# Cross-attention and a two-step mixture of experts on one core: the bias of the experts' second layer moved into a product tile, broadcast operands in place of diagonal matrices, idle products near the end, and a new order of work

## The reference

```python
logits = _gelu(xf @ w_r1 + b_r1) @ w_r2 + b_r2
top_p, top_i = jax.lax.top_k(jax.nn.softmax(logits, axis=-1), K)      # K = 2 of E = 8 experts
for _ in range(NUM_ITER):                                             # 2
    ctx = jnp.concatenate([integrated, v], axis=-1)
    shared_ctrl = _gelu(ctx @ w_s1 + b_s1) @ w_s2 + b_s2
    x_shared, v_shared = _inl(shared_ctrl, integrated, v, mu)
    hidden = _gelu(jnp.einsum('tc,tch->th', ctx_e, w1) + b1)          # w1, b1, w2, b2 of the token's experts
    ctrl = jnp.einsum('th,tho->to', hidden, w2) + b2                  # 64 hidden units, 384 outputs
    x_r, v_r = _inl(ctrl, x_e, v_e, mu)
    ...                                                               # weighted mean over the two experts
    halt = jax.nn.sigmoid(_gelu(x_next @ w_h1 + b_h1) @ w_h2 + b_h2)
    refined = _gelu(x_next @ w_f1 + b_f1) @ w_f2 + b_f2
    integrated = integrated + halt * refined * integration_weight
    v = v_next
```

## Time and profile before

| | us |
|---|---|
| median of 3 runs (lowest to highest) | 394.82 (390.18 to 397.71) |
| the profiled execution | 394.98 |
| its span, first to last instruction | 393.2 |
| PE busy | 352.4 (90%) |
| DVE busy | 294.6 (75%) |
| ACT busy | 255.3 (65%) |
| POOL busy | 47.0 (12%) |

### The profile page before, as it was taken

The page is one execution under the profiler, slowest core; times in us unless marked ns, Lnnn a source line. Parts: engine busy times, 40 slices in busy tenths (PEclk is TensorE's granted clock), DMA queues, the critical chain, the costliest instruction groups (busy, mean ns, idle before and its releaser), DMA issues. The chain is left out here.

```text
span 393.2 us, 5555 instructions
## 1 busy us (share of the span) xinstructions
PE 352.4 (90%) x1627; PEld 217.9 (55%) x1627; DVE 294.6 (75%) x649; ACT 255.3 (65%) x429; POOL 47.0 (12%) x57
## 2 busy tenths in 40 slices
PE   4778999998888978899998899999999999999775
PEld 2234444344333534566764657767767777776553
DVE  7587978768463468999998895985993995795822
ACT  2553576685858667896958767957686684786321
POOL 8029400024040403200000000000000000000000
PEclk9999999999999599999999999999999999999966
DMA  4540000000000000000000000000000000001000
GB/s 115 130 126 3 4 3 2 1 6 0 6 1 2 1 1 0 2 0 0 3 0 0 2 0 2 2 0 0 2 0 1 3 27 0 2 0 28 1 28 27
DMA packets 10667, 5.17 MB, mean 13 GB/s; under 512 B 4264, under 2 KB 10573, under 8 KB 10637
## 3 DMA queue, kind: packets, MB, share of 16 engines
q1 hardware_dynamic: 10637, 4.82, 4.6%
HBM read 3.64 MB, written 1.05 MB: 12 GB/s over the span
## 5 line engine op out<-in xcount | busy, mean ns | idle before, releaser
L674 PE MATMUL bank<-qs,w_hi 128*128 128x512 f32 x160 | 70.7, 442 | 0.0
L675 PE MATMUL bank<-qs,w_lo 128*128 128x512 f32 x160 | 63.1, 394 | 0.0
L850 ACT ACT_TABLE_LOAD x37 | 47.5, 1283 | 1.4 <-PEq L1346 0.7
L922 ACT ACTIVATE PT<-bank 77x512 f32<-77x512 f32 x64 | 35.4, 589 | 17.0 <-PE bank L779 9.6
L679 PE MATMUL bank<-KB,w_hi 128*128 128x512 f32 x160 | 43.7, 394 | 0.0
L961 ACT ACTIVATE hid<-bank,cols 128x512 f32<-128x512 f32 x40 | 27.0, 692 | 18.2 <-PE bank L640 18.0
L674 PEld LDWEIGHTS bank<-qs,w_hi 128*128 128x128 f32 x160 | 30.4, 190 | 7.8 <-ACT shared L967 1.0
L1234 DVE SCALAR_TENSOR_TENSOR masked<-Ib,cst,hid 128x512 f32<-128x512 bf16 x32 | 23.2, 750 | 15.1 <-ACT hid L961 15.1
L790 PE MATMUL bank<-PT,VO 77*32 77x512 f32 x256 | 34.3, 629 | 0.0
L679 PEld LDWEIGHTS bank<-KB,w_hi 128*128 128x128 f32 x160 | 30.0, 187 | 7.4
L675 PEld LDWEIGHTS bank<-qs,w_lo 128*128 128x128 f32 x160 | 30.1, 188 | 6.5
(11 more groups left out here) (230 smaller groups left out, 677.9 us busy)
## 6 DMA issues: line engine op xcount, KB each, us to landing
x_tok<-in_x_dram SPq DMA_DIRECT2D x4, 256.0 KB, 3.3
hid<-in_L_ffn_expert_w_dram SPq DMA_DIRECT2D x1, 768.0 KB
out_dram<-x_tok SPq DMA_DIRECT2D x3, 256.0 KB, 2.3
masked<-in_L_ffn_expert_w_dram SPq DMA_DIRECT2D x2, 256.0 KB
wf_sb<-in_L_ffn_w_f_dram SPq DMA_DIRECT2D x2, 128.0 KB
qs<-mT SPq DMA_DIRECT2D x16, 8.0 KB
out_dram<-x_tok SPq DMA_DIRECT2D x2, 128.0 KB, 1.8
hid<-in_L_ffn_w_s_dram SPq DMA_DIRECT2D x2, 96.0 KB
```

Source lines behind the costliest of these rows:

```text
L674: pe.matmul(t[:], lhsT=w2_hi[:, j, o:o + D], rhs=hi, start=False, stop=False)
L675: pe.matmul(t[:], lhsT=w2_lo[:, j, o:o + D], rhs=hi, start=False, stop=False)
L850: act.add_instruction(mybir.InstLoadActFuncSet(name=nc.get_next_instruction_name(), act_func_set_id=chosen, ins=[], outs=[]))
L922: step(act.activation(PT[0:KL, i % PT_TILES, :], ST[i % SCORE_BANKS][0:KL, :], ACT.Exp, scale=float(DH) ** -0.5))
```

## The change

In the second layer's weights the four tiles of eight experts become five, of which each slot uses four. Experts 1 to 6 keep three full tiles. Expert 7 goes to the lower half (rows 64 to 127) of tile HIGH, expert 0 to the upper half (rows 0 to 63) of tile LOW. The free halves hold the eight rows of the bias. The hidden tile has ones in those halves, and the mask turns them into the one-hot rows. Slot 0 uses HIGH, slot 1 uses LOW. For this the two experts of a token have to be sorted: expert 0 may stand only in slot 1, expert 7 only in slot 0. POOL swaps them on four numbers a token (`first`, `gap`). The product with `OH` and the making of `OH` and `b2_s` are gone. The first hidden tile is now read by two activations of 64 rows each (expert 7 to HIGH, expert 0 to LOW).

Instead of the diagonal matrices, PE takes as weights one number per token, repeated over 128 columns (`order_of`, `share_of`), and the identity as moving operand, 128 tokens at a time: four small products for one large. POOL has six operations on 4 or 8 columns a batch in place of four on 512.

Stage `hold` puts products of ones on PE after the last `w2`: 2, then 10 before the last `tail`, 1 before the last `fin`. They wait for `sp` and `gt` of (7, 1), since they write a bank that these read.

`x_lo` gets a tile of its own (`x_low`) and `fh` as well. Loads of the weights are cut in more pieces: 30 in place of 25 on one semaphore, 12 in place of 10 on another. The tables of places have new numbers.

```diff
@@ -61,10 +61,18 @@
-C_IDENT, C_EXPERT, C_ONEHOT, C_LO_Q, C_LO_K, C_SPLIT1, C_SPLIT2, C_RANK, C_END = 0, 128, 132, 133, 134, 135, 136, 137, 145
+C_IDENT, C_EXPERT, C_LO_Q, C_LO_K, C_RANK, C_END = 0, 128, 134, 135, 136, 144
+SHARED, HIGH, LOW = NK, 0, NK + 1
+def tile_of(slot, j):
+    return j if j else (HIGH, LOW)[slot]
...
-    ("w2", 2): (10.2, None, None, None), ("sp", 0): (None, -5.18, None, None), ("sp", 1): (None, 4.29, None, None),
+    ("w2", 2): (9.57, None, None, None), ("sp", 0): (None, -5.18, None, None), ("sp", 1): (None, 3.52, None, None),
...
+HOLD_AT = {
+    0: 195.5, 1: 197.0, 2: 198.0, 3: 202.0, 4: 215.66,
+}
+HOLD_PRODUCTS = {
+    0: 2, 1: 2, 2: 5, 3: 3, 4: 1,
+}
...
@@ -526,14 +540,19 @@
-            load(w2_in[:, 0:NK], e_w2.rearrange("(k e) h o -> (e h) k o", e=2), ffnw_in)
+            load(w2_in[:, 1:NK], e_w2[1:E - 1].rearrange("(k e) h o -> (e h) k o", e=2), ffnw_in)
+            load(w2_in[H:P, HIGH], e_w2[E - 1], ffnw_in)
+            load(w2_in[0:H, LOW], e_w2[0], ffnw_in)
+            load(w2_in[0:E, HIGH], e_b2, ffnw_in)
+            load(w2_in[H:H + E, LOW], e_b2, ffnw_in)
...
@@ -587,6 +606,8 @@
                     step(pool.tensor_tensor(w2_lo[H:P, NK], w2_lo[H:P, NK].bitcast(F32), w2_lo[H:P, NK].bitcast(F32), ALU.subtract))
+                    step(pool.memset(hid[0:H, HIGH, :], 1.0))
+                    step(pool.memset(hid[H:P, LOW, :], 1.0))
...
@@ -605,14 +626,15 @@
-                    for slot in range(2):
-                        w = wk[:, 4 + slot, :].unsqueeze(2).to_broadcast([P, NT, P])
-                        e = idxf[:, slot, :].unsqueeze(2).to_broadcast([P, NT, P])
-                        step(pool.tensor_tensor(diag_w[:, slot], eye, w, ALU.mult))
-                        step(pool.tensor_tensor(diag_i[:, slot], eye, e, ALU.mult))
+                    swap = first[:].unsqueeze(1).to_broadcast([P, 2, NT])
+                    step(pool.tensor_tensor(gap[:], chosen[:, :, 0], chosen[:, :, 1], ALU.subtract))
+                    pool.wait_ge(pool_done, n[0])
+                    step(pool.tensor_tensor(gap[:], gap[:], swap, ALU.mult))
+                    pool.wait_ge(pool_done, n[0])
+                    r = slice(NT * b, NT * (b + 1))
+                    for to, q in ((order_of, 0), (share_of, 1)):
+                        step(pool.tensor_tensor(to[:, 0, r], chosen[:, q, 1], gap[:, q], ALU.add))
+                        step(pool.tensor_tensor(to[:, 1, r], chosen[:, q, 0], gap[:, q], ALU.subtract))
...
@@ -661,7 +683,6 @@
                         if k > 0:
-                            pe.matmul(t[:], lhsT=b2_s[:, o:o + D], rhs=OH[:, k - 1, c, :], start=True, stop=False)
                             units = [(j, mask_hi[:, (k - 1) * NK + j, :], mask_lo[:, (k - 1) * NK + j, :]) for j in range(NK)]
...
+                elif stage == "hold":
+                    pe.wait_ge(act_done, act_at("sp", LAST, 1))
+                    pe.wait_ge(act_done, act_at("gt", LAST, 1))
+                    for i in range(HOLD_PRODUCTS[k]):
+                        pe.matmul(CT[0][0][:], lhsT=ones_bf[:], rhs=ones_bf[:].unsqueeze(1).to_broadcast([P, NT, P]), start=True, stop=True)
...
@@ -811,11 +838,11 @@
                 elif stage == "bc":
-                    pe.wait_ge(pool_done, pool_at("lgx", b, 0, k + 1))
-                    if k % 2 == 0:
-                        last = pe.matmul(t[:], lhsT=ones[:], rhs=diag_w[:, k // 2], start=True, stop=True)
-                    else:
-                        last = pe.matmul(t[:], lhsT=ones_bf[:], rhs=diag_i[:, k // 2], start=True, stop=True)
+                    pe.wait_ge(pool_done, pool_at("lgx", b))
+                    for i in range(NT):
+                        value, eye = ((share_of, ident), (order_of, ident_bf[:]))[k % 2]
+                        one = value[:, k // 2, NT * b + i:NT * b + i + 1].to_broadcast([P, P])
+                        last = pe.matmul(t[:, P * i:P * (i + 1)], lhsT=one, rhs=eye, start=True, stop=True)
...
@@ -958,7 +985,8 @@
                     for j in range(NK + 1):
                         t = await_product(act, (stage, s, j))
-                        step(act.activation(hid[:, j, :], t[:], ACT.Gelu, bias=cols[:, V_B1 + j:V_B1 + j + 1]))
+                        for rows, to in ((slice(0, P), j),) if j else ((slice(H, P), HIGH), (slice(0, H), LOW)):
+                            step(act.activation(hid[rows, to, :], t[rows, :], ACT.Gelu, bias=cols[rows, V_B1 + j:V_B1 + j + 1]))
...
-                elif stage == "bc" and k % 2:
-                    dve.wait_ge(act_done, act_at("bc", b, k))
-                    step(dve.tensor_scalar(OH[:, k // 2, b, :], Ib[:, k // 2, b, :], cst[:, C_ONEHOT:C_ONEHOT + 1], None, ALU.is_equal))
```

More of the change, by code:

```diff
@@ L76, in shape_constants @@
     c[:, C_IDENT:C_IDENT + P] = np.eye(P)
-    for k in range(NK):
-        c[:, C_EXPERT + k] = E - (2 * k + p // H)
-    c[:, C_ONEHOT] = np.where(p < 3 * E, E - p % E, -1)
+    for k in range(1, NK):
+        c[:, C_EXPERT + k] = E - (2 * k - 1 + p // H)
+    row = np.where(p % H < E, E - p % H, -1)
+    c[:, C_EXPERT + HIGH] = np.where(p >= H, 1, row)
+    c[:, C_EXPERT + LOW] = np.where(p < H, E, row)
     c[:, C_RANK:C_RANK + E] = E - np.arange(E)
@@ L144 @@
+HOLD_AT = {
[3 more added lines that the diff above has]
+    0: 2, 1: 2, 2: 5, 3: 3, 4: 1,
 }
 KEEP_AT = {
[L146 removed]
+    0: 76.19, 1: 68.42, 2: 101.37, 3: 69.61, 4: 87.18, 5: 83.1, 6: 81.05, 7: 126.89,
 }
 KEEP_PRODUCTS = {
[L149 removed]
+    0: 4, 1: 7, 2: 4, 3: 2, 4: 7, 5: 8, 6: 9, 7: 0,
 }
 SECOND_FFN = {
[L153 removed]
@@ L154 @@
-    ("mask", 1): {"dve": -12.72}, ("round", 2): {"act": -2.64}, ("low", 2): {"dve": -9.46}, ("round", 0): {"act": -2.37},
-    ("low", 0): {"dve": -1.99}, ("round", 1): {"act": -0.25}, ("low", 1): {"dve": 1.24}, ("w2", 0): {"pe": 6.96},
-    ("w2", 1): {"pe": 1.8}, ("w2", 2): {"pe": 8.18}, ("sp", 0): {"act": 7.43}, ("sp", 1): {"act": 1.92}, ("sp", 2): {"act": 8.35},
-    ("gt", 0): {"act": -2.56}, ("gt", 1): {"act": -1.59}, ("gt", 2): {"act": 4.2}, ("mix", 0): {"dve": 6.9},
-    ("mix", 1): {"dve": 8.3}, ("mix", 2): {"dve": -2.05}, ("tail", 0): {"pe": -0.23, "act": -0.66},
+    ("halves", 0): {"act": -11.31, "dve": 0.68}, ("w1", 0): {"pe": -3.01, "act": 0.03}, ("mask", 0): {"dve": 0.76},
@@ new lines @@
+    ("mask", 1): {"dve": -12.16}, ("round", 2): {"act": -2.64}, ("low", 2): {"dve": -4.88}, ("round", 0): {"act": -2.37},
+    ("low", 0): {"dve": -1.99}, ("round", 1): {"act": -0.25}, ("low", 1): {"dve": 1.24}, ("w2", 0): {"pe": 6.48},
+    ("w2", 1): {"pe": 1.8}, ("w2", 2): {"pe": 8.18}, ("sp", 0): {"act": 7.43}, ("sp", 1): {"act": 1.92}, ("sp", 2): {"act": 8.07},
+    ("gt", 0): {"act": -2.56}, ("gt", 1): {"act": -1.59}, ("gt", 2): {"act": 7.25}, ("mix", 0): {"dve": 9.82},
+    ("mix", 1): {"dve": 8.3}, ("mix", 2): {"dve": -1.84}, ("tail", 0): {"pe": -0.23, "act": -0.66},
@@ L221, in engine_order @@
     placed = [(at, key) for at, key in placed if key not in order and (key[0] != "fin" or key[1] >= NB)]
+    if engine == "pe":
+        placed += [(at, ("hold", 0, i)) for i, at in HOLD_AT.items() if HOLD_PRODUCTS[i] > 0]
     placed.sort(key=lambda item: item[0])
@@ L328, in xattn_moe_kernel @@
         ident_bf = sb("ident_bf", [P, P], BF16)
-        ones = sb("ones", [P, P])
         ones_bf = sb("ones_bf", [P, P], BF16)
@@ L373, in xattn_moe_kernel @@
         wk = sb("wk", [P, 6, NT])
-        idxf = sb("idxf", [P, 2, NT])
-        diag_w = sb("diag_w", [P, 2, NT, P])
-        diag_i = sb("diag_i", [P, 2, NT, P], BF16)
+        chosen = sb("chosen", [P, 2, 2, NT])
+        idxf = chosen[:, 0]
+        first = sb("first", [P, NT])
+        gap = sb("gap", [P, 2, NT])
         vec_rows = sb("vec_rows", [V_END, P])
@@ L678, in ffn_stage @@
                                 pe.wait_ge(dve_done, dve_at("low", s, k - 1, j + 1))
-                            last = pe.matmul(t[:], lhsT=w2_hi[:, j, o:o + D], rhs=lo, start=False, stop=(j == units[-1][0]))
+                            last = pe.matmul(t[:], lhsT=w2_hi[:, tile_of(k - 1, j), o:o + D], rhs=lo, start=False, stop=(j == units[-1][0]))
                         last.then_inc(stream_full, 1)
@@ L1192, in _ @@
                     step(dve.tensor_tensor(wk[:, 0, :], mx[:, 1, :], mx[:, 0, :], ALU.subtract))
+                    step(dve.tensor_tensor(first[:], idxf[:, 1, :], idxf[:, 0, :], ALU.is_gt))
                 elif stage == "lgx":
```

155 lines of the change are left out of this document (72 added, 83 removed), and 30 rows, old and new, of tables (BATCH_SHIFT, PLACES).

## The result

The change made the kernel slower. Its median is 400.89 us (399.73 to 404.11) against 393.81 for the kernel before; the ratio is 1.021, with a 95% interval of 1.014 to 1.028. Timed again it was 402.31, ratio 1.019 (1.012 to 1.026). The sign is clear; whether the loss is above 2% is not. The forecast was 384.7, and its range ended at 390.0.

The account below looks back on a forecast made before the run. PE, busy 90% of the span, was taken as the limit, alone in the second iteration and shared with DVE in the first. Terms -4.3 - 3.0 + 1.5 - 4.3 = -10.1 gave 384.7 us, range 379.5 to 390.0.

Parts of the forecast that it names:

- POOL's six small operations: Last router: copies of 32 columns take 0.16 us; with waits 0.35 each, about 2 us after 153.7, hidden before first `bc`.
- POOL's small operations wait for a mask each: Rival, last router: six waits of 0.7 us, slot 0 starts 1.9 later, 1.5 reach the end; 386.2 us, chance 0.12.
- The attention: Busy PE pays about +0.7, POOL's later start +1.0 at the first `pv`; sum +1.5 us (0 to +3.5).
- +1.0 at the first `pv`: Start of attention: POOL 2.4 us later from loads and splitting; copies ended at 45.5, PE used them at 46.98.
- The +0.7 forecast: Attention on PE: +0.1 for each pair of `bc`, two pairs a batch, three batches, and three products of ones.
- Last router and steps 0 to 3: After 149.09: PE's side -0.4 - 3.7 + 0.6 = -3.5, DVE's slack covers most; taken -3.0 us (-0.5 to -4.5).
- the second activation: Hidden tile 0 read twice: 0.33 us stop a step, +1.3 for four steps in second iteration; +0.6 in step 3.
- Second iteration: Steps 4 to 7: 24 bias products removed, -5.6 us; hidden tile read twice, +1.3; together -4.3.
- The end: Last tail: products of ones fill 2.6 of 3.86 us idle, clock stays up; -4.3 us (0 to -4.7).
- The rival of the falling clock: Last tail: the clock falls all the same, so the end's 4.3 us are lost; 389.0 us, chance 0.2.
- More spells at half clock in steps 0 to 3: Rival: PE stops oftener, each spell costs five us; two give 394.7, third 399.7, fourth 404.7; chance 0.08 for two or more.

Follow-up runs that it names:

- DVE's wait: Changed kernel with one wait added: DVE lets POOL finish batch 3's six small operations before step 0's second set of masks; 396.61 us, ratio 0.996.
- the pieces: Changed kernel with POOL's long subtraction (2304 columns) cut into six of 384; first `pv` at 49.7 us, where the change has 51.3; no total time given.

## Why the prediction was wrong

The forecast was -10.1 us and the spans differ by +9.0. Of these 19 us about 12 lie in the last router and steps 0 to 3, 5 in the attention, and 1 each in the second iteration and the end.

- **"POOL's six small operations have no row ... I take 0.35."** This is the step that failed: the six were to be done in about 2 us and took 7.7. It cost 6.5 us in the profiled pair, and 8.0 by what DVE's wait gives back: 5.5 of it a stop of PE, the rest products at half clock behind the stop. Alone one takes 0.20, even less than my 0.35; what runs beside them was not followed. I looked at the four masks that come next on DVE and stopped there. POOL got in at none of the boundaries between the eight subtractions behind them, and all four `bc` wait for all six operations. The rival "POOL's small operations wait for a mask each" had the place and the direction, at 1.5 us and a chance of 0.12: it priced one instruction of DVE's per operation of POOL's, where one operation waited for eight.
- **The attention: "+1.0 at the first `pv`".** It was +4.3. I followed the chain through POOL's copies of the values, and its terms were right: 2.4 later forecast, 2.5 measured. But the longer and later subtraction also covered an operation of DVE's that it had missed before, and the first `pv` hangs on DVE's chain: 2.6. The other 1.7 are a spell at half clock, which no term foresaw. The attention behind it costs +0.4 (84.6 in four variants of the change against 84.2 in the kernel before without bias products, all at the full clock there). The +0.7 forecast is near by luck: its own terms, six times 0.1 and three products of 0.22, come to 1.3, and those three stand in the last router's sum as well. The profiled execution shows +2.3 because the clock fell at 109 to 122 us.
- **Last router and steps 0 to 3: -3.0, ends -0.5 and -4.5.** Without the stop, in the run with DVE's wait, these stretches still take about 0.5 more than before, outside both ends. The kernel before without the products shows that they were worth 0.5 in steps 1 to 3, where PE's side of the sum had 2.8. And I charged the second activation in step 3 alone: there it costs 0.7, near the 0.6, but also 0.5 in each of steps 1 and 2. The new order, which had no term, costs 0.5.
- **Second iteration: -4.3.** Measured -3.5. The products gave 5.6 exactly; the second activation costs 1.7 where I took 1.3. The other 0.3 or so is not traced.
- **The end: -4.3.** Measured -2.9 and -3.4. The mechanism was right, and nine products instead of three ahead of the tail give 4.3. Three leave a gap of 1.5 us: of the nine traces of the change and its variants with three, the clock fell for 3.4 us of the tail in six and for 10.2 in three. The rival of the falling clock was partly right.
- **More spells at half clock in steps 0 to 3.** One came, behind the stop for POOL, and none in steps 1 to 3. The Trainium skill (TensorE: Matmul & The Clock Gate, A second HAM failure mode) tells of short stops that make the clock fall again and again; the four tails with nine holding products, at full clock up to PE's last product, with ACT between the products, do not show it.

The two stops look alike: an operation on four columns of one engine ends with the long work of the other. The Trainium skill (SBUF — State Buffer, Who interferes with whom) has DVE and GpSimd exclude each other for a whole instruction, when DVE's has two SBUF inputs and GpSimd's reads SBUF, or when DVE's runs in a two-port mode, which `tensor_scalar` can enter. At the start the traces agree: DVE's `tensor_scalar` of 2.96 us ends with POOL's instruction of 5.07; its mode no run shows. At the router my rival took that unit, one instruction for each operation, and the trace has POOL out for eight.

## What to carry over

When a small operation moves beside another engine that shares something with it, read not its next instruction but the whole row that follows, and test whether the small one gets in between: one operand decided it here. Then ask who waits for the small one. Products taken from an engine that is not the limit pay almost nothing (0.5 us for twelve), while an activation added on a path to the limiting engine pays nearly in full. Before a gain is put down to an edit, look whether the clock was the same in both traces: the pieces' 1.4 us were a spell that fell elsewhere. For a clock that falls in an idle gap, fill the gap to its end: three products left 1.5 us, and the gain came only in some executions.

## What the runs showed of the hardware

- A GpSimd operation on 4 columns took 5.52 us beside eight DVE instructions on two SBUF operands of 512 columns, 0.602 us apart, in all eight traces of that order; 0.71 when each also read a scalar column (0.665 apart); 0.20 with DVE idle. Why that read lets POOL in was not shown, nor whether the time between two instructions would alone.
- A DVE operation on 4 columns took 2.96 us beside a GpSimd subtraction of 2304 columns, 2.17 to 3.35 in eight traces, and ended with it each time. DVE's four statistics of `x_tok` beside the same subtraction took 0.86 us, as in the kernel before.
- With PE idle for 1.5 us and again for 0.8 ahead of the last tail the granted clock fell to 0.50 in nine traces of nine, for 3.4 or 10.2 us; with 0.2 and 0.8 it stayed at 1.00 to PE's last product in four of four.
